# A layer of scan, experts and attention on one core: the scan's step in full width instead of two halves

## What is computed

```
def step(s, t):
    x_t, b_t, c_t = t
    s = jnp.clip(s * A + b_t[:, None, :] * x_t[:, :, None], -10.0, 10.0)
    y = jnp.sum(c_t[:, None, :] * s, axis=-1)
    return (s, y)
_, ys = jax.lax.scan(step, s0, xs)
```

## Time and profile before

| | |
|---|---|
| median of three runs | 2550.72 us (2540.39 to 2566.41) |
| the profiled execution, its own time | 2556.13 us |
| its span, first to last instruction | 2554.1 us |
| TensorE (PE) busy | 2253.7 us, 88% |
| VectorE (DVE) busy | 1995.5 us, 78% |
| ScalarE (ACT) busy | 725.6 us, 28% |
| GpSimd (POOL) busy | 809.9 us, 32% |
| scan's multiplications, L1394 | 2048, busy 702.3 us |
| scan's additions, L1404 | 2048, busy 505.6 us |
| mean granted clock of TensorE | 0.875 |

### The profile page before, as it was taken

The page is one execution under the profiler, slowest core; times in us unless marked ns, Lnnn a source line. Parts: engine busy times, 40 slices in busy tenths (PEclk is TensorE's granted clock), DMA queues, the critical chain, the costliest instruction groups (busy, mean ns, idle before and its releaser), DMA issues. The chain is left out here.

```text
span 2554.1 us, 57186 instructions
## 1 busy us (share of the span) xinstructions
PE 2253.7 (88%) x16096; PEld 1916.9 (75%) x16096; DVE 1995.5 (78%) x6529; ACT 725.6 (28%) x1656; POOL 809.9 (32%) x1042
## 2 busy tenths in 40 slices
PE   7845877999999898989899898989898999989997
PEld 3422666888878787878788787878787887878887
DVE  3549856879797978889897989888888978798632
ACT  3430202223231423233232313132222323142323
POOL 0032203334231424333332424242333323142524
PEclk9855767989898988989898989989898989899988
DMA  7531000001010100010010101010000001010000
GB/s 268 176 107 24 23 10 18 11 11 27 8 26 10 27 10 23 11 25 12 13 25 7 27 11 27 11 27 11 23 11 18 20 11 24 9 27 6 6 1 9
DMA packets 101002, 73.43 MB, mean 29 GB/s; under 512 B 64376, under 2 KB 94592, under 8 KB 99712
## 3 DMA queue, kind: packets, MB, share of 16 engines
q1 hardware_dynamic: 100736, 70.08, 10.0%
HBM read 46.43 MB, written 23.59 MB: 27 GB/s over the span
## 5 line engine op out<-in xcount | busy, mean ns | idle before, releaser
L1394 DVE TENSOR_TENSOR decayed_state<-state,decay 128x128 f32<-128x128 f32 x2048 | 702.3, 383 | 1.0
L792 POOL TENSOR_TENSOR hs_parts<-hs_whole,hs_parts 128x256 fp32r<-128x256 f32 x640 | 488.0, 776 | 484.5 <-ACT hs_whole L916 464.6
L1404 DVE CUSTOM_DVE_ANT_0 state<-decayed_state,bank 128x128 f32<-128x128 f32 x2048 | 505.6, 285 | 34.0 <-PE bank L1006 16.2
L916 ACT ACTIVATE hs_parts<-bank,f_b_sb 128x256 fp32r<-128x256 f32 x512 | 244.8, 478 | 772.7 <-PE bank L1088 772.7
L1006 PE MATMUL bank<-xrows,brows 128*128 128x256 f32 x1024 | 261.0, 345 | 122.2 <-DVE state L1404 100.7
L1088 PE MATMUL bank<-f_w_hi,hs_parts 128*128 128x256 f32 x2048 | 348.0, 293 | 10.7 <-DVE x L1491 9.9
L1088 PEld LDWEIGHTS bank<-f_w_hi,hs_parts 128*128 128x128 f32 x2048 | 284.1, 193 | 52.7 <-ACT hs_parts L916 46.6
L1006 PEld LDWEIGHTS bank<-xrows,brows 128*128 128x128 f32 x1024 | 178.3, 216 | 178.8 <-DVE state L1404 92.2
L816 POOL TENSOR_TENSOR kv<-kv,kvm 128x272 f32<-128x272 f32 x64 | 48.8, 765 | 672.1 <-DVE kvm L1603 671.5
L916 ACT ACTIVATE hs_whole<-bank,f_b_sb 128x256 f32<-128x256 f32 x512 | 245.5, 480 | 0.0
L1088 PE MATMUL bank<-late_fT_parts,f_w_hi 128*128 128x256 f32 x1024 | 187.9, 317 | 0.5 <-DVE kvm L1603 0.5
(11 more groups left out here) (154 smaller groups left out, 3540.8 us busy)
## 6 DMA issues: line engine op xcount, KB each, us to landing
xrows<-xs_dram SPq DMA_DIRECT2D x512, 32.0 KB
brows<-bs_dram SPq DMA_DIRECT2D x1024, 2.0 KB
xt<-in_x SPq DMA_DIRECT2D x4, 1024.0 KB, 7.7
xn_dram<-xn SPq DMA_DIRECT2D x4, 1024.0 KB, 5.4
z_dram<-zT SPq DMA_DIRECT2D x4, 1024.0 KB, 4.1
f_w_sb<-in_f_w SPq DMA_DIRECT2D x2, 2048.0 KB
xs_dram<-xhi SPq DMA_DIRECT2D x4, 1024.0 KB, 4.5
xs_dram<-xlo SPq DMA_DIRECT2D x4, 1024.0 KB, 8.2
```

The source lines that it names most:

```text
L792: return pool.tensor_tensor(lo, whole, hi.bitcast(f32), ALU.subtract)
L916: act.activation(slot[:, m], HB[e % 2][:, m * TOK:(m + 1) * TOK], ACT.Relu, bias=g["f_b1"][:, e, m:m + 1]).then_inc(done.sem, 1)
L1394: dve.tensor_tensor(decayed_state[:, part], state[:, (s - 1) % RING, part], decay[:, part], ALU.mult).then_inc(decayed.sem, 1)
L1404: dve._custom_dve(add_sat, out=state[:, s % RING, part], in0=decayed_state[:, part], in1=U[n % 2][:, s % 2 * D + h * HALF:s % 2 * D + (h + ...
```

## The change

Each step of the scan becomes one multiplication and one addition over all 256 columns. The order is then multiply, add, multiply, add. The semaphores `decayed` and `stepped` count one per step instead of two, and the waits of TensorE on `stepped` are rewritten to the same points of the scan. Nothing else is moved.

```diff
@@ the counts
-        decayed = signal("decayed", 2 * CT)
-        stepped = signal("stepped", 2 * CT, before=2)
+        decayed = signal("decayed", CT)
+        stepped = signal("stepped", CT, before=1)
@@ scan_inputs, scan_output on TensorE
-                    pe.wait_ge(stepped.sem, stepped.after(i, 4 * (n - 1)))
+                    pe.wait_ge(stepped.sem, stepped.after(i, 2 * (n - 1)))
-                pe.wait_ge(stepped.sem, stepped.after(i, 8 * (quad + 1)))
+                pe.wait_ge(stepped.sem, stepped.after(i, 4 * (quad + 1)))
@@ start
-            dve.memset(decayed_state[:, 0:HALF], 0.0).then_inc(stepped.sem, 1)
-            dve.memset(decayed_state[:, HALF:D], 0.0).then_inc(stepped.sem, 1)
+            dve.memset(decayed_state[:], 0.0).then_inc(stepped.sem, 1)
@@ scan_pair on VectorE
                 for s in (2 * n, 2 * n + 1):
-                    for h in range(2):
-                        part = slice(h * HALF, (h + 1) * HALF)
-                        dve.wait_ge(stepped.sem, stepped.after(i, 2 * (s - 1) + h + 1))
-                        dve.tensor_tensor(decayed_state[:, part], state[:, (s - 1) % RING, part], decay[:, part],
-                                          ALU.mult).then_inc(decayed.sem, 1)
+                    dve.wait_ge(stepped.sem, stepped.after(i, s))
+                    dve.tensor_tensor(decayed_state[:], state[:, (s - 1) % RING, :], decay[:],
+                                      ALU.mult).then_inc(decayed.sem, 1)
                     if s == 2 * n:
                         dve.wait_ge(u_made.sem, u_made.after(i, n + 1))
                         ...
-                    for h in range(2):
-                        part = slice(h * HALF, (h + 1) * HALF)
-                        wait_apart(decayed, decayed.after(i, 2 * s + h + 1))
-                        dve._custom_dve(add_sat, out=state[:, s % RING, part], in0=decayed_state[:, part],
-                                        in1=U[n % 2][:, s % 2 * D + h * HALF:s % 2 * D + (h + 1) * HALF],
-                                        s0=LIMIT, s1=-LIMIT).then_inc(stepped.sem, 1)
+                    wait_apart(decayed, decayed.after(i, s + 1))
+                    dve._custom_dve(add_sat, out=state[:, s % RING, :], in0=decayed_state[:],
+                                    in1=U[n % 2][:, s % 2 * D:(s % 2 + 1) * D],
+                                    s0=LIMIT, s1=-LIMIT).then_inc(stepped.sem, 1)
```

More of the change, by code:

```diff
@@ L39 @@
 KERNEL_EPS = 0.001
-HALF = D // 2
 def constants():
```

## The result

The changed kernel takes **2624.87 us** (median of 4 runs, 2616.42 to 2629.55), the kernel before, on the same chip, 2546.90 (2540.39 to 2566.41). The ratio is **1.029, 95% interval 1.022 to 1.036**: slower, and outside the range of 2515 to 2585. The profiled execution's own time is 2620.41 us, its span 2617.7.

The account below looks back on a forecast made before the run. It took a relay between VectorE and TensorE to bound the kernel, VectorE deciding in two stretches. -14 us over 14 chunks and +8 for the first gave -6 on 2556.1, so 2550, median 2545 us; range 2515 to 2585.

Parts of the forecast that it names:

- The price of a step: VectorE's scan: an undisturbed merged step takes 1.01 us, or 1.10 with the other waits, instead of 0.83 or 0.91.
- the dearer of the two waits of the earlier trace: The addition's separate wait for its multiplication: 0.14 us, or 0.23 with the pair's other waits behind it.
- The rival that waits are free: Third rival: waits in series cost VectorE nothing, giving 2481 us; chance 0.03.
- Collisions: Scan multiplications held by GpSimd on the shared port: 12.8 us a chunk lost, 8.5 taken as saved.
- 1391 to 1290 of the next chunk ... Net -0.3: Gating, normalization, routing, where VectorE decides: 8 pairs cost +2.3 us, collisions saved offset it, net -0.3 a chunk.
- 2.3 saved: Collision saving in the stretch before the routing: 2.3 us a chunk of 4.1 lost there.
- the two thirds: Share of the multiplications' collision loss with GpSimd taken as saved by merging: 8.5 us a chunk.
- The rest, 13 pairs, mostly attention: ... hidden in front of 1390.61: Attention pairs: +3.4 - 1.3 us a chunk on VectorE, costing nothing because its 2.58 us lead covers them.
- if the attention stretch starts to make TensorE wait: One of the named signs that would show the forecast wrong; it concerns the attention, with no size given.
- First chunk: Scan alone with GpSimd idle: four pairs take 8.44 us instead of 7.09, +1.35 for six groups, +8 us.
- three stretches: The chunk's split: 1391 to 1290 (8 pairs), 1295 to 1335 (9), the rest (13); together -1.0 us a chunk.
- Rival 1: GpSimd's operations land on the next multiplication, so the collision saving falls to none: 2608 us; chance 0.22 with half-way cases.

Follow-up runs that it names:

- e12: Kernel before with full width in pairs 30, 31 and 0 to 5 alone (the scan's share before the routing): 2570.24 us, ratio 1.012.
- e1: Kernel before with full width in pairs 18 to 29 alone, those in the attention: 2602.02 us, ratio 1.024.
- e7: Changed kernel with TensorE's scan product among the numerators made one head later: 2603.34 us, ratio 1.024 to the kernel before.
- e10: Kernel before, halves in all pairs, only TensorE's scan product among the numerators moved one head later: 2572.14 us, ratio 1.011.
- e11: Kernel before with full width in pairs 20, 21, 26 and 27 alone and TensorE's scan product one head later: 2608.5 us, ratio 1.026.
- e6: Kernel before with full width only in pairs 20, 21, 26 and 27, run next to the numerators: 2632.33 us, ratio 1.035.
- e9: Kernel before, halves in all pairs, only TensorE's scan product among the numerators moved one head earlier: 2586.41 us, ratio 1.018.
- e4: Changed kernel with GpSimd's splitting of hidden activations cut to 8 of 256 columns: 2511.96 us, ratio 0.990 to the kernel before.
- e2: Kernel before with full width in the 20 pairs outside the attention, halves in pairs 18 to 29: 2556.94 us, ratio 1.007.
- e3: Kernel before (halves) with GpSimd's splitting of hidden activations cut to 8 of 256 columns: 2455.61 us, ratio 0.967.
- e5: Kernel before with full width everywhere but in pairs 20, 21, 26 and 27: 2565.28 us, ratio 1.009.
- e8: Kernel before with full width in pairs 0, 8 to 12, 15 and 16 alone: 2531.83 us, ratio 0.994.

## Why the prediction was wrong

*The price of a step: right.* Four pairs of the first chunk take 229.71 - 221.18 = 8.53 us (8.44 forecast, 7.09 before), the median instruction is 0.425 (0.42), and L1398 waits for its own L1390 63.9 us over 272 times, 0.23 each, the dearer of the two waits of the earlier trace rows. The rival that waits are free is out. The Trainium skill, "VectorE: DVE Perf Modes", section "The DRAIN you can't avoid", reports that a chain of copies takes the same time with a semaphore after each as with one after the last. The trace doesn't agree for this chain; these 63.9 us speak against it.

*Collisions: 94 us of 203 saved, 7.4 of 12.8 in the chunk, where I took 8.5.* The size was nearly right and the split by stretches wrong. Among the experts 5.0 us a chunk were saved (4.1 forecast), but that stretch can give back only what TensorE waits there, and its later waits did shrink (1.06 to 0.57).

*First failing step: "1391 to 1290 of the next chunk ... Net -0.3".* The term mis-sized is "2.3 saved"; the windows show 4.1 - 3.7, some 0.4, and the stretch became 1.1 us a chunk longer (40.75 to 41.81) in place of 0.3 shorter. VectorE's and GpSimd's timelines of the changed kernel at the stretch's worst pair, 31, show what stayed:

```profile
1288.37 1.50 DVE L1390 TENSOR_TENSOR decayed_state<-state,decay 128x256 f32<-128x256 f32 x1
1290.10 0.42 DVE L1398 CUSTOM_DVE_ANT_0 state<-decayed_state,bank 128x256 f32<-128x256 f32 x1 [0.23 <-DVE decayed_state L1390]
1290.56 1.44 DVE L1390 TENSOR_TENSOR decayed_state<-state,decay 128x256 f32<-128x256 f32 x1
```
```profile
1288.12 1.46 POOL L879 TENSOR_TENSOR mb<-mb,a_t 128x512 f32<-128x512 f32 x1
1290.43 1.29 POOL L791 TENSOR_TENSOR late_fT_parts<-late_turn,late_fT_parts 128x512 fp32r<-128x512 f32 x1 [0.84 <-ACT late_fT_parts L907]
```

Two operations of GpSimd, 512 wide, 1.46 and 1.29 us, start 0.25 and 0.13 us ahead of a multiplication's start, and each holds that one multiplication until 0.29 and 0.28 us past its own end. The pair loses 1.50 + 1.44 - 2 x 0.425 = 2.1 us. The same two met the same pair in the kernel before, where each held one pair of halves:

```profile
1254.51 1.56 DVE L1394 TENSOR_TENSOR decayed_state<-state,decay 128x128 f32<-128x128 f32 x2
...
1256.51 1.58 DVE L1394 TENSOR_TENSOR decayed_state<-state,decay 128x128 f32<-128x128 f32 x2
```

That is 1.56 + 1.58 - 2 x 0.48 = 2.2 us. Each of these operations, alone as they stand, costs VectorE 1.0 to 1.1 us at either width. I had taken the two thirds from rows 6 and 7, with operations of 0.74 us back to back, where the second half was held a second time; that pattern is the experts', not this stretch's. What remains here is mainly the wider steps, and TensorE's wait for comb grows by 14.0 us over the trace. e12 gives the stretch 1.2%, where the prediction had a gain of 4 us.

*Second failing step, the larger: "The rest, 13 pairs, mostly attention: ... hidden in front of 1390.61".* It is hidden there: VectorE waits longer at that point than before, 3.04 against 2.58. But I asked only what VectorE is late for at the stretch's end, not who reads the state inside it. TensorE asks for it twice among the numerators. Before, it found it ready; with pairs 0.26 us longer it waits 0.25 and 0.31. By the wait alone that is 0.56 x 15 = 8 us. e1 measures 2.4%, 64 us. Of the rest, 32.6 us are numerators and kv at the lower clock for longer (31.0 in the changed kernel), which go with the waits by e7, e10 and e11 set against the changed kernel, before and e6. By the same runs a third to a half of the change's cost is there without the waits. e12's relay is part of it; how four wider pairs in the attention cost 1.5% without a wait there (e11 against e10) is open. The prediction named the sign, "if the attention stretch starts to make TensorE wait", and gave it no price.

The Trainium skill, "TensorE: Matmul & The Clock Gate", section "A second HAM failure mode: psum-queue depth-cycling", tells of a kernel in which short idle times between groups of matmuls make the clock swing between its two levels. The traces agree in part: with waits of 0.25 to 0.7 us, 264 to 266 us for numerators and kv (changed, e1, e6, e9) and 252 in e4; with none and the product in its place, 222 to 241 (before, e2, e3, e5, e8, e12). Idle time is not all of it, since e10 reaches 254 us with no wait. Where the product of width 256 stands among numerators of width 17 matters too.

*First chunk: right*, (8.53 - 7.09) x 6 = 8.6 us against 8; its scan as a whole took 90.5 us in place of 82.4. It ended only 1.2 us later than before, because it began 6.9 us earlier in the profiled execution (its first addition at 173.4 us in place of 180.3; at 180.3 in e1 and 175.6 in e12), for a reason that was not looked for.

*A slip in the sum*: its three stretches have 8 + 9 + 13 = 30 pairs and 8.1 us of the 32 pairs and 9.0 us. At 0.26 us each the two pairs left out are at most 7 us over 14 chunks, a tenth of the miss.

*The rivals.* Rival 1 has the sign and nearly the time, 2608, but mostly by luck: it was to decide below a third of the collisions saved, and 46% were, and most of the loss lies in the attention, where it had none. In front of the routing alone it was near the mark, with next to nothing saved.

In sum, by the profiled spans, +63.6 us: 31.0 numerators and kv at the lower clock, 3.4 other matmuls, 14.0 comb, about 8 for the two new waits, 8.6 for the first chunk, which leaves an idle remainder of -1.4. This says where the time lies, and not that each term has a cause of its own.

## What to carry to other kernels

Slack at the end of a stretch covers an engine only if nobody reads its intermediate results inside; before costing an edit at nothing, look up every wait of TensorE on that engine and how much margin each has. A new wait of a quarter of a microsecond between small matmuls can go with a loss of several times its length by the granted clock, and so can a matmul moved among them without any wait, so compare TensorE's busy time for the same instructions, not its idle time alone. And when a saving comes from chance meetings of two engines, split it by stretches: here nearly half of it was saved, mostly where it couldn't be cashed. Last, when a run moves an instruction to make a wait or to remove one, run the move without the wait too: here it had a price of its own.

## What the runs showed of the hardware that was not expected

Moving one product of two matmuls by one head among the numerators, with no edit elsewhere, costs 1.8% (earlier, with waits) or 1.1% (later, without one). The 16 numerators behind it take 1.85 or 3.60 us by the granted clock (1.00 or 0.50), and two groups of matmuls that never changed range from 222.1 to 266.4 us over the runs, 1.7% of the kernel's time.
